# Half-slot loads, a head-interleaved scratch layout, and attention's full-width products gathered in three units of a block

## The reference, cut to what matters

```python
qkv = x @ qkv_w + qkv_b                       # x here is layernormed
allowed = (dist > 0) & (dist <= w) & (k_gpos[:, None, :] >= 0)      # w = 128
attn = jax.nn.softmax(jnp.where(allowed, scores, NEG), axis=-1)
local = jnp.einsum('bhnqk,bhnkd->bhnqd', attn, vb)
...
lattn = jax.nn.softmax(lscores, axis=-1)      # 64 chunk means, 4 heads
remote = lat_out @ rout_w + rout_b
gate = jax.nn.sigmoid(local @ gl_w + remote_h @ gr_w)
mixed = gate * local + (1.0 - gate) * remote_h
return mixed @ out_w + out_b
```

## Time and profile before

| | us |
|---|---|
| median of 3 runs (683.4 to 690.52) | 685.05 |
| the profiled execution's own time | 687.44 |
| its span, first to last instruction | 685.6 |
| TensorE, VectorE, ScalarE, GpSimd busy | 558.6, 407.7, 288.9, 238.4 |
| granted TensorE clock, mean over the span | 0.898 |

### The profile page before, as it was taken

One profiled execution on the slowest core, in us unless ns is written; L12 is line 12 of the kernel. 1 busy time (PEld: TensorE's weight loads), 2 busy tenths in 40 slices (PEclk: granted clock), 3 DMA queues, 4 the chain that ended last, 5 costly groups with the idle time before them and its releaser, 6 DMA issues. The chain is left out here.

```text
span 685.6 us, 28265 instructions
## 1 busy us (share of the span) xinstructions
PE 558.6 (81%) x11345; PEld 391.0 (57%) x11345; DVE 407.7 (59%) x2034; ACT 288.9 (42%) x787; POOL 238.4 (35%) x465
## 2 busy tenths in 40 slices
PE   7887545979599598697685895898789999999992
PEld 3544212757477376475564674676536777667772
DVE  6684424557367386276464465477656467667655
ACT  2353200657367376276464464487512221221110
POOL 5545100134235243153243233245531243342342
PEclk9999867799799799599799698599999999999998
DMA  3474532111202102002002012000000000000001
GB/s 77 133 212 154 173 111 83 41 61 44 78 6 64 58 13 78 36 22 90 15 28 90 8 32 88 5 6 6 3 0 1 1 2 15 15 15 16 17 15 31
DMA packets 28506, 33.30 MB, mean 49 GB/s; under 512 B 5852, under 2 KB 22212, under 8 KB 28380
## 3 DMA queue, kind: packets, MB, share of 16 engines
q1 hardware_dynamic: 27324, 31.20, 14.6%
q10 hardware_dynamic: 1056, 0.35, 0.2%
HBM read 19.93 MB, written 11.27 MB: 46 GB/s over the span
## 5 line engine op out<-in xcount | busy, mean ns | idle before, releaser
L1088 DVE CUSTOM_DVE_ANT_0 added<-psS,maskq 128x160 bf16<-128x160 f32 x512 | 157.1, 316 | 147.6 <-PE psS L936 87.9
L1291 ACT ACTIVATE probs<-psST 128x512 f32<-128x512 f32 x256 | 152.7, 604 | 157.1 <-PE psST L967 154.3
L967 PE MATMUL psST<-qst,kst 98*32 98x128 bf16 (+3 forms) x2048 | 86.9, 207 | 5.6 <-issue 5.4
L981 PE MATMUL psPV<-probs,vst 128*9 128x128 f32 x1984 | 88.0, 289 | 2.2 <-issue 2.2
L963 PE MATMUL psST<-qst,kst 98*32 98x32 bf16 (+3 forms) x1920 | 83.6, 207 | 5.1 <-issue 5.0
L1263 POOL TENSOR_TENSOR gated<-both,glr 128x256 f32<-128x256 f32 x32 | 23.5, 733 | 143.0 <-DVE both L1189 143.0
L933 PE MATMUL psS<-kst,qst 68*32 68x96 bf16 (+3 forms) x512 | 24.3, 231 | 57.7 <-DMA rqT<-rq_t 48.8
L1724 ACT ACTIVATE hT<-fpsH 128x512 f32<-128x512 f32 x32 | 19.1, 598 | 121.6 <-PE fpsH L1468 121.6
L930 PE MATMUL psS<-kst,qst 68*32 68x160 bf16 x1536 | 67.0, 241 | 3.3 <-issue 2.3
L963 PEld LDWEIGHTS psST<-qst,kst 98*32 98x32 bf16 x1920 | 60.2, 101 | 6.5 <-issue 6.5
L951 PE MATMUL psST<-maskk,identb 128*32 128x128 bf16 x960 | 60.9, 231 | 0.3 <-issue 0.3
(11 more groups left out here) (183 smaller groups left out, 1237.7 us busy)
## 6 DMA issues: line engine op xcount, KB each, us to landing
q_parts<-split SPq DMA_DIRECT2D x24, 128.0 KB, 2.7
k_parts<-split SPq DMA_DIRECT2D x24, 128.0 KB, 2.7
qst<-q_parts SPq DMA_DIRECT2D x32, 96.0 KB
kst<-k_parts SPq DMA_DIRECT2D x32, 96.0 KB
v_tok<-vt SPq DMA_DIRECT2D x8, 288.0 KB, 2.6
vst<-v_tok SPq DMA_DIRECT2D x8, 288.0 KB
X<-in_L_attn_x_dram SPq DMA_DIRECT2D x8, 256.0 KB, 3.2
qst<-q_parts SPq DMA_DIRECT2D x32, 64.0 KB
```

What stands on the lines that cost most here:

```text
L967: last = nc.tensor.matmul(bank[quad(j), a, P + QD * j:2 * P], part(kst, KALL, n, h, QD * j, QD), part(qst, KALL, n, h, QD * j, P - QD * j) ...
L981: last = nc.tensor.matmul(psPV[32 * t:32 * t + VW, G * P:(G + 1) * P], vst[:, (n - 1 + side).mod(RING), 4 * G + t, :], probs[:, unit, (2 * ...
L1088: taken = nc.vector.tensor_tensor_reduce(added[:, h], psS[g % 2][:, a, 0:WIN], mask, 1.0, NEG * 4, ALU.add, ALU.max, rowmax[:, n.mod(2), h ...
L1291: nc.scalar.activation(probs[:, g], psST[g % 2][:].rearrange("p a c -> p (a c)"), ACT.Exp, scale=SCALE).then_inc(s_exp.sem, 1)
```

## The change

**Loads and layout.** The columns of the q and k weights are reordered once at the start by ScalarE (`wqk`), so that a projected row is (dimension, head), not (head, dimension); the biases are loaded in the same order. The scratch becomes [chunk, part, 128, 512], and the three parts of a side are stored by one DMA instead of three. The load of a chunk is made in halves of 8 heads (`load_half`): 3 DMAs for q, 4 for k, with rows of 8 KB, whose source and destination both begin with the row dimension (24, 16 or 8 rows; which of q and k repeats is exchanged). Each half has its own semaphore, for which TensorE waits at unit 0 and at unit 4; v and the latent query have a third one, for which it waits only at step 4c. Half 0 is issued in step 4(c - 1), half 1 a step later. Chunk 1 is now loaded in `project`, by k = 2 and 3. TensorE's wait for the constants of `attend` moves behind the first scores.

**Gathering.** The full-width products of a block stand in three units, each behind a `values`: unit 1 (`psM`, `psLP`), unit 3 (`psLS`, `psRem`, `psMix`), unit 5 (`pvs` to `psC`, then the projection, into a bank of its own half, `psProj` in `psB`). The copies on ScalarE and the small steps on VectorE and GpSimd move with them: on VectorE most by one unit, on ScalarE the copy of the maxima to unit 1, that of the latent probabilities behind `pvs` in unit 2, the latent exponentials to units 5 and 6, and the gate's exponential into unit 0 of the next step.

```diff
-HG = 4
-STORES = 16 * 8
-LOADS = 6 * H // HG + 2
-RUNS = ((0, 3), (3, 2), (5, 1))
+HALF = H // 2
+STORES = 16 * 4
+RUNS_Q = ((0, 0, 3), (3, 0, 2), (5, 0, 1))
+RUNS_K = ((0, 0, 1), (1, 0, 1), (2, 0, 2), (4, 1, 2))
+LOADS = 16 * (len(RUNS_Q) + len(RUNS_K))
...
+def load_half(sp, c, half, side, held, scratch, s_half):
+
+    u, heads = c % SLOTS, slice(half * HALF, (half + 1) * HALF)
+    tile, runs = ((held.qst, RUNS_Q), (held.kst, RUNS_K))[side]
+    rows = scratch[side][c].rearrange("a (d h) t -> (a d) h t", h=H)[:, heads].rearrange("r h t -> r (h t)")
+    for first, part, parts in runs:
+        sp.dma_start(tile[first * HD:(first + parts) * HD, u, heads].rearrange("r h t -> r (h t)"),
+                     rows[part * HD:(part + parts) * HD]).then_inc(s_half[half][u], 16)
...
-        q_parts = nc.dram_tensor("q_parts", [3, NCH, HD, H, CH], BF16, kind="Internal").ap()
-        k_parts = nc.dram_tensor("k_parts", [3, NCH, HD, H, CH], BF16, kind="Internal").ap()
+        q_parts = nc.dram_tensor("q_parts", [NCH, 3, P, CH], BF16, kind="Internal").ap()
+        k_parts = nc.dram_tensor("k_parts", [NCH, 3, P, CH], BF16, kind="Internal").ap()
...
-                    for part in range(3):
-                        sp.dma_start(parts[part, c.k].rearrange("d h t -> h d t"),
-                                     split[:, u, side, part]).then_inc(s_out[u], 16)
+                    sp.dma_start(parts[c.k].rearrange("a p t -> p a t"), split[:, u, side]).then_inc(s_out[u], 16)
...
                 if k == 2:
-                    sp.wait_ge(s_clear_late, 2)
+                    sp.wait_ge(s_clear_late, 1 + 2)
...
-                for hg in range(2 * k, 2 * k + 2) if k < 2 else ():
-                    load_q(sp, 0, hg, held, scratch, s_load)
-                    load_k(sp, 0, hg, held, scratch, s_load)
-                if k == 1:
-                    load_rest(sp, 0, held, scratch, s_load)
+                for side in range(2):
+                    load_half(sp, k // 2, k % 2, side, held, scratch, s_half)
+                if k % 2:
+                    load_rest(sp, k // 2, held, scratch, s_rest)
...
+            for side in range(2):
+                nc.scalar.activation(wqk[:, side].rearrange("k (d h) -> k d h", h=H),
+                                     wqkv[:, side * D:(side + 1) * D].rearrange("k (h d) -> k d h", h=H),
+                                     ACT.Copy).then_inc(s_lanes, 1)
...
@@ attend, SyncE @@
-            for hg in range(H // HG):
-                load_q(sp, 1, hg, held, scratch, s_load)
-                load_k(sp, 1, hg, held, scratch, s_load)
-            load_rest(sp, 1, held, scratch, s_load)
...
+                half = s.mod(LC) if s.live and 2 <= c < NCH and s.mod(LC) < 2 else None
+                if half is not None:
+                    sp.wait_ge(s_ST.sem, s_ST.after(s - 1))
+                    load_half(sp, c, half, 0, held, scratch, s_half)
...
+                if half is not None:
+                    if half == 0:
+                        sp.wait_ge(s_ST.sem, s_ST.after(s, HALF // 2))
+                    load_half(sp, c, half, 1, held, scratch, s_half)
+                if half == 1:
                     sp.wait_ge(s_pv.sem, s_pv.after(s - 1))
-                    paced(s, 5)
-                    load_rest(sp, c, held, scratch, s_load)
+                    load_rest(sp, c, held, scratch, s_rest)
...
@@ attend, TensorE @@
-            pe.wait_ge(s_consts, CONSTS)
...
-                        if g == 0 and n.mod(LC) == 0:
+                        if g % (HALF // 2) == 0 and n.mod(LC) == 0:
                             c = n.k // LC
-                            pe.wait_ge(s_load[c % SLOTS], 16 * LOADS * (c // SLOTS + 1))
+                            pe.wait_ge(s_half[2 * g // HALF][c % SLOTS], LOADS * (c // SLOTS + 1))
...
-                    if g == 0 and (s - 1).live:
+                    if g == 1 and (s - 1).live:
+                        values(s - 1, 3)
+                    if g == 1 and (s + 1).live:
+                        n = s + 1
+                        pe.wait_ge(s_neg.sem, s_neg.after(n))
+                        pe.wait_ge(s_y.sem, s_y.after(s - 3))
+                        nc.tensor.transpose(psM, mparts[:, n.mod(2)].rearrange("p a h -> p (a h)"),
+                                            identb[:]).then_inc(s_mT.sem, 1)
+                    if g == 1 and (s - 1).live:
...
-                    if g == 2 and s.live:
+                    if g == 3 and s.live:
+                        values(s, 0)
+                    if g == 3 and s.live:
...
+                    if g == 3 and (s - 1).live:
+                        n = s - 1
+                        pe.wait_ge(s_lpTc.sem, s_lpTc.after(n))
+                        pe.wait_ge(s_local.sem, s_local.after(n - 1))
...
-                    if g == 4 and (s - 1).live:
+                    if g == 5 and s.live:
+                        values(s, 1)
+                    if g == 5 and (s - 1).live:
                         n = s - 1
                         pe.wait_ge(s_pvs.sem, s_pvs.after(n))
                         pe.wait_ge(s_remote.sem, s_remote.after(n))
...
-                    if g == 6 and (s - 2).live:
+                    if g == 5 and (s - 2).live:
                         n = s - 2
                         pe.wait_ge(s_mixTc.sem, s_mixTc.after(n))
-                        pe.wait_ge(s_local.sem, s_local.after(n + 1))
-                        nc.tensor.matmul(psC[:, 0:D], mixedT[:], wout[:], start=True,
+                        nc.tensor.matmul(psProj, mixedT[:], wout[:], start=True,
...
@@ attend, ScalarE @@
-                    if g == 2 and (s + 1).live:
+                    if g == 1 and (s + 1).live:
                         n = s + 1
                         act.wait_ge(s_mT.sem, s_mT.after(n))
-
+                        act.wait_ge(s_lpT.sem, s_lpT.after(s - 1))
...
                         nc.scalar.activation(pvs[:, n.mod(2)], psPV[:], ACT.Copy).then_inc(s_pvs.sem, 1)
+                        act.wait_ge(s_lpT.sem, s_lpT.after(n))
+                        act.wait_ge(s_rem.sem, s_rem.after(n - 1))
+                        nc.scalar.activation(lprobT[:].rearrange("p f q -> p (f q)"), psLP,
+                                             ACT.Copy).then_inc(s_lpTc.sem, 1)
...
-                    if g in (4, 5) and s.live:
+                    if g in (5, 6) and s.live:
...
-                    if g == 7 and (s - 1).live:
-                        n = s - 1
+                    if g == 0 and (s - 2).live:
+                        n = s - 2
                         act.wait_ge(s_z.sem, s_z.after(n))
```

139 lines of the change are left out of this document (48 added, 91 removed).

## The result

The changed kernel takes **663.0 us** (median of 4 runs, 660.0 to 666.9) against 684.6 us of the kernel before on the same chip: ratio 0.967, 95% interval 0.960 to 0.975. It is faster by 22 us where 48 were forecast. The time lies in the forecast range, but less than half of the forecast gain is there.

A forecast was written before the change was run, and what follows sets the result against it. Bound: TensorE's waits for chunk loads in attention (48.8 us) and the low clock behind them. Profiled: 687.4 - 18 - 4 - 9.5 - 21.4 + 4 = 638.5; the median lies 2.4 lower, so 637 us, range 598 to 677.

The forecast's parts named there:

- the one from the quiet block to 28 blocks: Attention blocks 1 to 28: one block's 10.9 us plus 0.25 of short gaps, 11.15 us for each of 28.
- the chain of the quiet block: One gathered attention block followed through its waits, with nothing else happening: 10.9 us against 8.4 before.
- The loads alone would give some 100 us: Whole kernel: new loads without gathering gain some 100 us; the gathering takes more than half of it back.
- The base, 9.6 us for a block without a stall: Attention before the change: 16 blocks without a stall take 9.6 us each, 8.4 plus about 1.1 of gaps and slower units.
- Projection: Projection stage: ScalarE's 17.5 us of waits for stores go and SyncE issues less; gain 18 us, bounds 12 and 22.
- so many DMAs fewer to issue: SyncE in projection: with some 20 us less to issue, it ends about as much earlier.
- The low clock of step -2: Start of attention: if TensorE's idle gap ahead closes, step -2's 8 units lose 4 us, bounds 0 and 5.
- The maxima's DMA: Start of attention: chunk 1's DMAs no longer stand ahead of it; 8.2 us of wait plus 1.3 of low clock, 9.5.
- The end of attention: After block 28: block 29 and the longer tail of dependent steps cost 4 us.
- Gathering is harmless: Rival, attention blocks: the gathering's waits are covered, blocks take 9.25 us, total 579 us; chance 0.13.
- The clock falls in the waits: Rival, attention blocks: idle TensorE keeps the clock at 1.2 GHz, 13.6 us a block, total 704 us; chance 0.07.
- The loads still come late: Rival, attention loads: a wait in SyncE's stream holds the second half, 48.8 us stays, total 686 us; chance 0.04.

The follow-up runs named there:

- e1: The changed kernel with its loads, layout and projection, but attention's products in the order of the kernel before (no gathering): 635.1 us, ratio 0.924.
- e5: e1 with the q and k DMAs of a half spread, one behind each unit, instead of in two bursts: 622.0 us, ratio 0.912.
- e13: e1 with the spread loads of e5 and the later chunk 1 loads of e8, no gathering: 617.1 us, ratio 0.899.
- e8: e1 with half 1, v and latent query of chunk 1 loaded at the start of attention instead of the end of projection: 629.1 us, ratio 0.918.
- e4: The changed kernel without the loads of chunks 2 to 7 and TensorE's waits for them, for timing alone: 655.1 us, ratio 0.957.
- e6: e1 without the loads of chunks 2 to 7 and the waits for them, for timing alone: 614.3 us, no ratio.
- e2: The kernel before with only the gathering; loads, layout and projection as before: 718.1 us, ratio 1.050.
- e12: The changed kernel with the latent scores (psLS) back in unit 2: 644.7 us, ratio 0.947.
- e11: The changed kernel with ScalarE's copy pvs moved ahead of the copy of the maxima in unit 1: 647.7 us, ratio 0.949.
- e9: e5 with four filler products of 512 columns ahead of the values of unit 1 in each block: 626.7 us, ratio 0.915.
- e14: e5 with 40 more TensorE waits a block on a constant long reached, five in every unit: 667.0 us, ratio 0.977.
- e15: The changed kernel with the same 40 added waits a block as e14: 691.9 us, ratio 1.010.

## Why the prediction was wrong

**The step that failed** is the one from the quiet block to 28 blocks: "Of the 1.1 of short gaps I keep 0.25, since they fall partly into the new waits: 11.15." 28 blocks at 11.15 were 312.2 us, they took 325.0. By its terms: the chain of the quiet block was 0.3 us too long (10.60 against 10.9), which gives 8.4 us back; the gaps were 15.8 us where 7.0 were kept, 8.8 more; and 12.4 us came from blocks at a low clock or with longer units, for which the sum had nothing. The step took the issue gaps for short pauses that waits swallow. They are a limit of their own: they come behind TensorE's packets of instructions, grow with bursts of loads (e1, e5, e13 against e8), and all but vanish without them where the block is 10.6 us long (e4), but not where it is 8.5 (e6).

The same step makes "The loads alone would give some 100 us" wrong, and there the missing term is another. The base, 9.6 us for a block without a stall, of which 1.1 gaps and slower units, was read rightly: e1 has 1.13 us of gaps a block, and its blocks at a clock of 1.00 take 9.49. The stall didn't hide the gaps; their rows stood in the profile of before. What the sum lacked is that ten of e1's 28 blocks fall to clocks between 0.67 and 0.91 and take 12.84, where the 16 blocks of before had kept 0.99 on average. That makes 10.69 a block instead of 9.6, and 51 us instead of 100. Why a gap lowers the clock in one block and not in another no run shows: a gap of 2.6 us left block 2 of the kernel before at 1.00, and one of 2.6 stands in block 2 of e1, at 0.67.

**The other error had the opposite sign.** I priced the gathering at more than half of the loads' gain, over 50 us; it costs 28 (e1 against after). Its chain was right in its first waits: values of unit 3 wait 0.93 us for `pvs` (0.9 forecast), unit 5 waits 0.45 for `remote` (0.5), unit 3 takes 3.51 (3.3), unit 5 2.22 (2.4). The other two were too long: 0.7 for the maximum (0.85) and 0.2 for its parts (0.4). But only part of what a longer block adds is lost. The quiet block grows by 2.05 us, 57 over the stage, and the stage by 25.8: gaps fall from 31.6 us to 15.8, and what slow blocks and longer units cost from 28.2 to 12.4.

**By the terms of the sum** (638.5 against 666.9 for the profiled execution, 28.4 us too low): the 28 blocks are 12.8 of it. Projection gave 11.8 instead of 18 (6.2), and only 4 to 10 in the eleven other profiles of the same projection. The step "so many DMAs fewer to issue" was right, SyncE had issued all at 77.5 us, and ScalarE's waits for the stores fell from 17.5 to 4.8, not to none. But then SyncE waited until 83.5 for stores held up by chunk 1's loads; the change moves these loads ahead of the barrier, and I counted only their issue, not their traffic (e8). The low clock of step -2 stayed, since TensorE stood as long as before ahead of it: 10.39 us at 0.54, a forecast gain of 4 turned to -0.5 (4.5). The maxima's DMA gave 10.9 instead of 9.5 (-1.4, in steps -1 and 0). The end of attention cost 10.3 instead of 4 (6.3). It is the gathering's: that stage takes 53.1 and 53.0 us in e2 and e4 too, at a clock of 0.81 in e2, and 42.0 to 44.5 in the runs without gathering. The 4 us were no chain of waits but a guess at the tail.

**The rivals.** "Gathering is harmless" is out: it costs 34 us on the old loads (e2), and e12 and e11 get 15 to 18 us by mending one wait. "The clock falls in the waits" was right in kind and far too large: e4, nearly without gaps, still has a clock of 0.94, and e9 shows a stage at 1.00 where fewer waits and gaps are left; but 21 of the 28 blocks of the kernel after are at 1.00, and no kernel here was low in most of its blocks. "The loads still come late" is out; TensorE never waits for them. The stall went, at a DMA share of 0.9 in the bursts, as forecast.

**Open.** What sets the 3.3 us between two packets of instructions isn't settled. The records of e6 show what the distance is made of at its 21 gaps: the packet itself 0.9 to 1.4 us, 1.2 to 1.5 from its end to TensorE's next matmul, and 1.1 to 1.7 from there to the start of the next packet; what each of the three waits for they don't say. Open too are what lets the clock fall, why e14 showed three packets more and not seven, where 14 of its 43.6 us went, and how much of e15's 29 us is the clock.

## What to carry to other kernels

Read the rows named issue as a possible limit, with the queue of instructions beside them, and look block by block at what the blocks without a stall do: before a stall is taken out, ask what all blocks would cost at that rate, and how many of them would run at a low clock, since a mean over the quiet ones has no term for it. Where the engine is near its supply of instructions, added array time was nearly free (e9) and added waits were dear (e14), so count instructions, and spread bulk loads over the step even when there is room for a burst. A chain of waits that is right for one block in the middle prices neither the slow blocks nor the end of the stage. And a load moved to an earlier place costs more than its issue: whoever waits for a landing in the same stretch waits for its bytes too.

## What the runs showed that I had not expected

- TensorE's program came in packets of 16 KB over the queue q8, at 2.5 a block of 637 recorded matmuls and weight loads, in e5 and e6 never closer than 3.3 us; each of the 265 issue gaps over 0.5 us in blocks 1 to 28 of the eighteen profiles ended 1.1 to 1.9 us behind a packet's end.
- 25 us of filler work spread over 28 blocks cost 2.6 us of the stage (e9); 40 long satisfied waits a block cost 43.6 (e14), of which 14.9 are gaps.
- A store of 64 KB landed after 11.0 us, where the median of its line is 3.9, with 1.5 MB of loads around it; in twelve profiles with these loads the last such store took 11.0 to 13.8, in the two without them 3.8.
- The first scores of one and the same projection stood between 85.7 and 93.0 us in twelve profiles, so one profile's time of that stage decides little.
